# A router with its weights stationary on four column quarters, prefix ranks in PSUM, a bias added in place, and another order of steps in a gated cross-attention and expert layer

## The reference

```python
x = x + tanh(g_xattn) * xattn(ctx, layernorm(x), mask, ...)
x = x + tanh(g_ffn) * ffn(layernorm(x), w_router, w1, b1, w2, b2)
# xattn
q = ln @ Wq.T
kv = concatenate([xn @ Wkv.T, ln @ Wlkv.T], axis=1)
qn, kn = rmsnorm(q, qn_g) * SCALE, rmsnorm(k, kn_g)
attn = softmax(where(mask, einsum('bhid,bhjd->bhij', qn, kn), -max))
out = einsum('bhij,bhjd->bhid', attn, v) @ Wo.T + bo
# ffn
probs = softmax(xf @ w_router)
topk_w, topk_idx = top_k(probs, 2)
weights = sum(topk_w[..., None] * one_hot(topk_idx, 8), axis=1)
h = gelu(einsum('te,ieh->tih', xf, w1) + b1)
out = sum((einsum('tih,ihe->tie', h, w2) + b2) * weights[..., None], axis=1)
```

## Time and profile before

| | us |
|---|---|
| median of 3 runs | 1027.05 |
| lowest and highest | 1022.74, 1029.36 |
| profiled execution | 1023.27 |
| its span, first to last instruction | 1021.7 |
| its mean granted TensorE clock | 0.944 of full |

### The profile page before, as it was taken

One profiled execution on the slowest core, in us unless ns is written; L12 is line 12 of the kernel. 1 busy time (PEld: TensorE's weight loads), 2 busy tenths in 40 slices (PEclk: granted clock), 3 DMA queues, 4 the chain that ended last, 5 costly groups with the idle time before them and its releaser, 6 DMA issues. The chain is left out here.

```text
span 1021.7 us, 19903 instructions
## 1 busy us (share of the span) xinstructions
PE 890.3 (87%) x6028; PEld 682.5 (67%) x6028; DVE 625.9 (61%) x1497; ACT 544.4 (53%) x1439; POOL 351.8 (34%) x271
## 2 busy tenths in 40 slices
PE   4899989898898978989772099999999999999990
PEld 3644445454454645545342099999999999999990
DVE  5566676656766476564966156676757657757650
ACT  3777755856658566475513035454546445546430
POOL 2333232322655225552162422423323423333221
PEclk8999999998999899999995599999999999999996
DMA  4301000210002210010032342525252534342325
GB/s 124 126 1 44 2 0 20 68 40 2 32 32 67 79 42 32 32 63 1 16 110 71 107 129 41 134 45 130 44 136 41 134 46 129 54 126 42 50 32 174
DMA packets 49215, 66.31 MB, mean 65 GB/s; under 512 B 7409, under 2 KB 42993, under 8 KB 49105
## 3 DMA queue, kind: packets, MB, share of 16 engines
q0 software_dynamic: 17520, 33.27, 14.8%
q1 hardware_dynamic: 29296, 30.18, 10.0%
q10 hardware_dynamic: 2352, 2.31, 0.8%
HBM read 41.54 MB, written 28.39 MB: 68 GB/s over the span
## 5 line engine op out<-in xcount | busy, mean ns | idle before, releaser
L500 POOL TENSOR_TENSOR rr<-ssm,minus_half 128x4 f32<-128x4 f32 (+1 forms) x72 | 121.7, 1690 | 290.5 <-DVE ssm L791 290.5
L1615 PE MATMUL psH<-xT_hi,Q 128*128 128x256 f32 x1120 | 203.9, 281 | 1.6 <-DVE xT_lo L1532 1.6
L1628 PE MATMUL psY<-K,g_hi 128*128 128x256 f32 x1120 | 203.4, 284 | 0.0
L1468 POOL DMA_INDIRECT total<-y_out,token_i x70 | 115.0, 1643 | 255.4 <-DVE y_out L1553 243.9
L665 ACT ACTIVATE p_ring<-psS,shift 128x1024 f32<-128x1024 f32 x128 | 137.1, 1111 | 104.2 <-PE psS L1263 104.1
L1615 PEld LDWEIGHTS psH<-xT_hi,Q 128*128 128x128 f32 x1120 | 174.5, 190 | 2.0 <-issue 2.0
L1628 PEld LDWEIGHTS psY<-K,g_hi 128*128 128x128 f32 x1120 | 171.7, 188 | 0.0
L1628 PE MATMUL psY<-K,g_lo 128*128 128x256 f32 x560 | 157.3, 281 | 0.0
L1615 PE MATMUL psH<-xT_lo,Q 128*128 128x256 f32 x560 | 157.2, 281 | 0.0
L1279 PE MATMUL psO<-p_ring,V 128*64 128x512 f32 x576 | 151.5, 623 | 0.8 <-ACT o_sb L653 0.8
L827 DVE TENSOR_TENSOR p_sum<-p_sum,p_ring 128x1024 f32<-128x1024 f32 (+1 forms) x112 | 136.5, 1219 | 2.2 <-ACT p_ring L665 1.4
(11 more groups left out here) (238 smaller groups left out, 1248.7 us busy)
## 6 DMA issues: line engine op xcount, KB each, us to landing
lnf<-routed SPq DMA_DIRECT2D x35, 258.0 KB
xr<-in_L_ffn_w POOLq DMA_DIRECT2D x7, 1024.0 KB, 6.3
xn<-in_L_ffn_w POOLq DMA_DIRECT2D x7, 1024.0 KB, 8.7
xr<-in_x SPq DMA_DIRECT2D x8, 512.0 KB, 4.8
xb<-in_x SPq DMA_DIRECT2D x4, 1024.0 KB, 6.2
total<-xb SPq DMA_DIRECT2D x4, 1024.0 KB, 4.5
routed<-pad_rows SPq DMA_DIRECT2D x8, 258.0 KB, 4.4
total<-y_out,token_i POOLq DMA_INDIRECT x70, 3.9
```

The source lines that it names most:

```text
L500: pool.tensor_tensor(rr[0:p, c % 2, n], ssm[0:p, c % 2, n], minus_half[0:p, n], ALU.pow).then_inc(rr_ready, 1)
L1468: pool.indirect_dma_start(total, bass.IndirectOffsetOnAxis(ap=token_i[:, m:m + 1], axis=0), y_out[:, m, :], None, bounds_check=NTOK + TM - ...
L1615: ins = pe.matmul(o, l, r, start=(n == 0), stop=(n == len(parts) - 1))
L1628: ins = pe.matmul(psY[m][:, 0:D], l[:, c, cols], r[:, c, :], start=(c == 0 and n == 0), stop=(c == HC - 1 and n == 2))
```

## The change

- The bias `bo` is no longer a third matmul in `project_out` (`bo_pick`, `bo_cut`). `tbo` = gate x bias row is made once, and `residual_base(b, half)` adds it to `xb` on VectorE in steps 7 and 8 of window 2b.
- The router's weights, padded to 32 columns, are the stationary side; `yT` moves, 256 columns at a time, into the four 32-partition quarters of a bank. ScalarE copies the result (`take_logits`), TensorE turns it back (`turn_logits`, "lt").
- `ranks` adds the prefix over the tiles in PSUM with eight more small matmuls; `base` holds the region's start from the outset, and `router_slots` has 5 operations instead of 14.
- The second turn of a step and "lt" (but for the last window) go to bank 7; its readers and the sums' share one count. In the tail, banks 0 to 5 are used.
- Steps: logits, lt, ranks at steps 1, 2, 6 of windows 3 and 5 (0, 1, 4 in window 7), and the loops of VectorE, ScalarE and GpSimd accordingly. `second_offsets`, `norm_offsets` and `second_stats` now stand behind `scale_heads`, `norm_lo` ahead of `quotients`; `norm_stats`, `norm_variance`, `norm_root` one window's half earlier; scatters at steps 7, 8 and then 0 to 5 (window 7: all from step 5).

The diff, cut to its core:

```diff
-            router = sb("router", [P, EC, NE])
+            router = sb("router", [P, EC, BLOCK])
...
             def late_uses(w, i):
...
+                if w % 2 == 0 and b >= 1 and i in (7, 8):
+                    return [("turn", b - 1, 2 * (i - 7) + 1)]
+                if w % 2 == 1 and b >= 1:
+                    last = b + 1 == B
+                    if i == (0 if last else 1):
+                        return [("logits", b - 1)]
+                    if i == (1 if last else 2):
+                        return [("lt", b - 1)]
+                    if i == (4 if last else 6):
+                        return [("ranks", b - 1)]
...
+            tail_banks = (0, 1, 2, 3, 4, 5, 2, 3, 0, 1, 0)
...
+                    for name in late_uses(w, i):
+                        apart = name[0] == "turn" or name[0] == "lt" and name[1] + 2 < B
+                        yield 7 if apart else g % 2, name
...
             def _(pool):
...
+                        if b == 0 and i == 4:
+                            norm_root(1)
                         if b >= 1 and i == 5:
                             second_root(b - 1)
-                        if b >= 2 and i < 5:
-                            scatter(b - 2, 6 + 2 * i, 2)
+                        if b >= 2 and i < 6:
+                            scatter(b - 2, 4 + 2 * i, 2)
+                    elif b >= 1:
+                        if b + 1 == B:
+                            if i >= 5:
+                                scatter(b - 1, (i - 5) * 4, 4)
+                        elif i >= 7:
+                            scatter(b - 1, (i - 7) * 2, 2)
+                    if w % 2 == 1 and i == 8 and b + 2 < B:
+                        norm_root(b + 2)
...
+                def residual_base(b, half):
...
+                    dve.tensor_tensor(xb[:, b % 2, t, :], xb[:, b % 2, t, :], tbo[:].unsqueeze(1).to_broadcast([P, HT, D]),
+                                      ALU.add).then_inc(xb_ready, 1)
...
                 def router_slots(b):
...
-                    for t in range(T):
-                        dve.tensor_tensor(base[:, t + 1, :], base[:, t, :], bank(name)[:, D + t * NE:D + (t + 1) * NE],
-                                          ALU.add).then_inc(base_ready, 1)
-                        dve.wait_ge(base_ready, b * (T + 2) + (t + 1))
+                    then_step(dve.tensor_tensor(slot[:], bank(name)[:, 0:T * NE].rearrange("p (t e) -> p t e", t=T),
+                                                base[:].unsqueeze(1).to_broadcast([P, T, NE]), ALU.add))
...
+                    last = b + 1 == B
+                    if not even and past and i == (5 if last else 7):
+                        router_slots(b - 1)
+                    if not even and past and last and i == 3:
+                        router_softmax(b - 1)
+                    if not even and past and last and i == 4:
+                        router_largest(b - 1, 1)
+                        router_rows(b - 1)
                     if g >= 1:
                         add_probabilities(2 * g - 2)
-                    if even and past and i == 6:
-                        second_offsets(b - 1)
-                    if even and more and i == (5 if b == 0 else 2):
-                        norm_offsets(b + 1)
...
                     if tile_at(g) is not None:
                         scale_heads(tile_at(g))
 
+                    if not even and more and i < 5:
+                        norm_lo(b + 1, i)
+                    if even and past and i == 6:
+                        second_offsets(b - 1)
+                    if even and more and i == (5 if b == 0 else 0):
+                        norm_offsets(b + 1)
                     if i == 1 and w >= 1:
                         quotients(2 * w - 1)
                     if i == 6:
                         quotients(2 * w)
...
+                    if even and i in (7, 8):
+                        residual_base(b, i - 7)
...
+                    if not even and b + 2 < B:
+                        if i in ((2, 3) if b == 0 else (0, 2)):
+                            norm_stats(b + 2, i - 2 if b == 0 else i // 2)
+                        if i == 8:
+                            norm_variance(b + 2)
...
+                    if not even and past and not last:
                         if i == 4:
+                            router_softmax(b - 1)
+                            router_largest(b - 1, 0)
+                        if i == 5:
+                            router_largest(b - 1, 1)
                             router_rows(b - 1)
...
-                    for t in range(T):
-                        ins = passes(bank(name)[:, t * NE:(t + 1) * NE], [(yT[:, c, t * P:(t + 1) * P], router[:, c, :]) for c in range(EC)])
+                    for c in range(EC):
+                        for j in range(4):
+                            ins = pe.matmul(bank(name)[j * BLOCK:(j + 1) * BLOCK, 0:2 * P], router[:, c, :],
+                                            yT[:, c, j * 2 * P:(j + 1) * 2 * P], start=(c == 0), stop=(c == EC - 1))
                     ins.then_inc(logits_done, 1)
...
-                    pe.matmul(bank(name)[:, D:D + T * NE], ones[:], chosen[:], start=True, stop=True).then_inc(rank_done, 1)
+                    pe.matmul(bank(name)[:, 0:(T + 1) * NE], tri[:], chosen[:], start=True, stop=False)
+                    for t in range(T):
+                        behind = bank(name)[:, (t + 1) * NE:(T + 1) * NE].rearrange("p (t e) -> p t e", e=NE)
+                        ins = pe.matmul(behind, ones[:], chosen[:, t * NE:(t + 1) * NE].unsqueeze(1).to_broadcast([P, T - t, NE]),
+                                        start=False, stop=(t == T - 1))
...
-                        ins = passes(bank(name)[:, n * D:(n + 1) * D], [(att[:, c, t * P:(t + 1) * P], wo[:, c, :]) for c in range(EC)]
-                                     + [(bo_pick[:], bo_cut[:])])
+                        ins = passes(bank(name)[:, n * D:(n + 1) * D], [(att[:, c, t * P:(t + 1) * P], wo[:, c, :]) for c in range(EC)])
```

More of the change, by code:

```diff
@@ L691, in _ @@
                         turned_rows(b - 1, 3)
-                    if w % 2 == 1 and b >= 1 and i == 2:
-                        router_exp(b - 1)
+                    last = b + 1 == B
+                    if w % 2 == 1 and b >= 1 and i == (1 if last else 2):
+                        take_logits(b - 1)
                     for u in (2 * g, 2 * g + 1):
@@ L1298, in use @@
                 def use(name):
-                    kind = {"wo": turn_output_weights, "norm": turn_norm, "out": project_out, "turn": turn_rows, "logits": logits, "ranks": ranks}[name[0]]
+                    kind = {"wo": turn_output_weights, "norm": turn_norm, "out": project_out, "turn": turn_rows, "logits": logits, "lt": turn_logits,
+                            "ranks": ranks}[name[0]]
                     kind(*name[1:])
```

172 lines of the change are left out of this document (84 added, 88 removed).

## The result

The changed kernel takes 998.97 us (median of 4 runs, 997.54 to 1001.87), the kernel before 1024.89 on the same chip (1021.34 to 1029.36): ratio 0.9748, 95% interval 0.9699 to 0.9797. The forecast was 1008, range 993 to 1020. The profiled execution took 997.54 us (span 996.0), 25.7 less than the one of before; the sum had said 17.6.

What follows compares the result with a forecast made beforehand. TensorE was taken to bound the attention stage, partly set by a chain through other engines to `qkd`; gains and losses summed to -17.6 us, taking 1025.6 to 1008 us, range 993 to 1020.

Steps and rivals of the forecast that it cites:

- Bias: Projection in steps 0 to 3 of windows 2, 4, 6, and tail: bias matmuls of 0.31 us go; -7.4 and -2.5 us.
- Router: Router bursts in three windows: 4.1 to 2.1 us each, -6.0 us; added turns and rank matmuls, +2.7 us.
- Clock: TensorE behind the router and the wait for `chosen` in three windows: stretches at half clock go, -12 us.
- `chosen`, `K`, `ln_lo`: TensorE waits in the attention stage: 10.1 us for `chosen` and 2.2 for `K` go, 2.0 net for `ln_lo`.
- Even windows: Windows 2, 4, 6: scatters ahead of the heads' root and late `second_offsets` delay steps 7 and 8; +13.1 us.
- Window 0: Window 0: `norm_offsets(1)` behind `scale_heads` holds `norm_rows`, and `tbo` additions cost at window 1's start; +2.8 us.
- Windows 3 and 5: Steps 6 to 8 there: softmax, maxima and `router_slots` on VectorE lengthen the chain to `qkd`; +7.1 us.
- GpSimd: Roots on GpSimd beside VectorE's `tbo` additions: contention could cost 0.9 us eight times, 7 us; none counted.
- Tail: Behind the attention stage: 2.5 us saved by the bias, 1.1 by shorter `router_slots` less the ranks.
- New waits are not met: Attention stage: ScalarE and VectorE recover within slack, losses shrink from 23 us to some 5; 990 us, chance 20%.
- Router quarters don't overlap: Router product: quarters run one after another (4.2 us), TensorE still falls to 1.2 GHz; 1024 to 1026 us, chance 15%.
- Slower: Windows 4 and 6: scatters ahead of the root and late `second_offsets` cost 16 us more each; 1040 us, chance 4%.

Runs made afterwards that it cites:

- 7.2 by the experiment: Changed kernel with the bias row back in project_out as a third product and no residual_base; 8.6 us more than the changed kernel by the medians.
- 6.2 us by the experiment: Changed kernel with the router product as before (yT stationary, 32 small matmuls, no copy or turns of logits); median 14.1 us above the changed kernel's.

## Why the prediction came out as it did

The direction, the mechanism of each gain and the places of most losses were right; the time was 9 us too high. The tail gave 4.4 more than its terms, the router 3.6 more, the even windows lost 2.8 less, start and experts gave 2.0 without cause; `chosen`, the clock and a missed wait took 4 to 5 of it back. So the total is nearer than its terms are, by errors that cancelled in part. Of the signs named ahead, the 16 router instructions, the missing `bo_cut` and an attention stage between 450 and 470 us (459.7) came; the burst is 1.0 us and not 2, a wait for `chosen` stays in window 7, the wait for `qkd` is 14.5 us in all and not above 16.5, and half clock is as frequent as before, in other places.

- **Bias.** 24 x 0.31 = 7.4 in the windows: 7.2 by the experiment, but as nine steps of mostly 0.82 and three of next to nothing. That the number is met is luck: the slot was too small and the wait for `xb` took the difference back. In the tail 3.9 instead of 2.5: the term took the bias matmul's own slot and left out that the `wo` matmuls run closer without it.
- **Router.** From 4.1 to 2.1 us: it went from 3.67 (twice) and 4.08 to 1.00, 8.4 saved and not 6.0. The factor of two was the wrong one of the two bounds. From start to start the two turns take 0.37 and the nine rank matmuls 0.32 us, the two of before 0.18: 1.5 for three windows, not 2.7.
- **Clock.** -12.0: the stretches behind the router are gone and were worth 6.2 us by the experiment (7.4 said). But the stage has as much of 1.2 GHz as before, 30.7 us both times. 20.5 of them now stand in step 7 of windows 2 to 6 (the last of it in step 8 of window 2), where the new waits are, and some 7 at the start and in step 6 of window 0. The step that failed is the 1.0 and 0.5 us that the forecast allowed for the clock behind its own new waits. They cost some 5 us in steps 7 and 8 of windows 2 to 6, an estimate from kernels in which no 1.2 GHz fell there: step 7 of window 2 takes 9.76 us in three of them, and steps 7 and 8 of window 3 take 7.9 and 5.3, instead of 10.69 and of 9.30 and 4.88. Two of the stretches, windows of the changed kernel, columns of the earlier trace rows:

```profile
256.97:260.38 3.41, 3.17 (x10) 2.12 (x12) 2.41 (x7) 0.85 (x8) 0.00 (x0) 0.50 0.00 0
...
441.29:448.11 6.82, 4.93 (x13) 1.32 (x12) 4.40 (x9) 6.39 (x20) 1.92 (x1) 0.50 0.01 2
```

- **`chosen`, `K`, `ln_lo`.** 12.3 + 2.0: `chosen` gave 7.3, since in window 7 TensorE still waits 2.8 us. `ln_lo` and `K` in windows 1, 3 and 5 were 7.6 us of waits and are 5.1, all of them for `K`: 2.5 gained where 4.2 were counted. The forecast said that the route "starts as soon as VectorE may"; it does, and VectorE is what window 7 waits for, as the kernel with the later ranks showed.
- **Even windows.** +13.1: the wait at step 7 came as described (3.14 for `qkd`, then `K`) and `normed_rows` idled for 5.3 us, 5.9 said. Step 7 is 1.7, 3.3 and 4.6 us longer in windows 2, 4 and 6, step 8 0.6 in window 2 and nothing in the others: 10.2. The forecast followed the queue of ScalarE into step 8, where it was no longer late. About 3 of the 10.2 us are the clock's. The cause was half named: in windows 4 and 6 the landing of the scatters held the rows as much as `second_offsets`.
- **Window 0.** +2.8: +3.2 there, by `norm_offsets` as said; window 1 gave 1.5 back.
- **Windows 3 and 5.** +7.1: the route on VectorE was to lengthen `qkd` in steps 6 to 8. It did not (step 8 of window 3 is 1.9 us shorter than before); step 7 lost 3.6 and 3.8 us by the bank of the ranks, which the forecast did not have: 2.28 are the wait, most of the rest the clock.
- **GpSimd.** The forecast counted no root lengthened by the additions of `tbo`, and rightly: none of the eight runs beside an instruction of GpSimd.
- **Tail.** -3.6: -8.0 measured. 3.9 the bias, 1.7 the slots (1.1 said), 1.5 in router, turns and clock, 1.0 in the sixteen scatters (21.2 instead of 22.2 us).
- **Rivals.** "New waits are not met": they are met, idle time is as before. "Router quarters don't overlap": they do. "Slower": no step lost more than 4.6 us.

## What to carry over

When an operation is moved, look also at what its buffer holds up: the reader of a PSUM bank and the scatter that still reads a row are part of the step. When a wait is removed on an engine that is filled by a chain through four others, expect the idle time to stay until the chain itself is shortened or spread; here it fell from 43.2 us to 37.1 when the second norm's chain began a step earlier, to 39.5 when VectorE's two long jobs were put in different steps, and to 34.0 with both. When the waits of two executions are compared, look at the clock of the work ahead of each: the same release after `qkd` left 1.57 us idle behind work at 1.2 GHz and 2.69 behind work at 2.4. A small matmul beside large ones can cost half as much again as its own slot; compare the spacing of its neighbours with and without it.

## What was not expected of the hardware

- Four 32-column quarters with one stationary matrix each run fully at once: 16 fp32 instructions of 256 columns in 1.0 us, 0.2 us for each four, in either order of the loops.
- `wo` instructions of 128x256 in fp32 are 0.22 us apart alone and 0.27 with a 64-row matmul after every fourth.
- After the same idle time of 3.41 us in step 7 of window 6 and 2 of one kernel (scatters in steps 0 to 3), the granted clock of the step is 1.00 in one and 0.85 in the other; a wait does not always cost the clock. Why, these runs don't show.
